# Moving the routing of token runs 0 to 2 from the first expert stage into the last slots of the attention ahead of it

## The reference, cut to what matters

```python
# attention, 8 sequences of 256 tokens, 16 heads of 8
scores = einsum('bhql,bhkl->bhqk', q, k) / sqrt(8)
scores = where(q_ind < k_ind, NEG_INF, scores)
ctx = einsum('bhqk,bhkl->bhql', softmax(scores), v)   # then @ out_w + out_b
# expert layer: x is normed first; every expert is silu(h @ g.T) * (h @ u.T) @ d of width 352
logits = x @ wr.T + rb                                # 7 routed experts
scores, idx = top_k(softmax(logits), 2)
scores = scores / scores.sum(-1)
out = shared_expert(x) + sum_e w[e] * expert_e(x)
```

## Time and profile before

| what | value |
|---|---|
| median of 3 runs | 1063.21 us (1061.97 to 1065.6) |
| span of the profiled execution | 1093.7 us |
| its own time beside the span | none is given; the span stands 30.5 us over the median |
| PE, DVE, ACT, POOL busy | 87%, 67%, 51%, 43% of the span |
| attention of layer 0 | 0 to 182.2 us |
| expert stage of layer 0, last slot starts | 182.2 us, 349.8 us |

### The profile page before, as it was taken

One profiled execution on the slowest core, in us unless ns is written; L12 is line 12 of the kernel. 1 busy time (PEld: TensorE's weight loads), 2 busy tenths in 40 slices (PEclk: granted clock), 3 DMA queues, 4 the chain that ended last, 5 costly groups with the idle time before them and its releaser, 6 DMA issues. The chain is left out here.

```text
span 1093.7 us, 24314 instructions
## 1 busy us (share of the span) xinstructions
PE 946.4 (87%) x8249; PEld 744.2 (68%) x8264; DVE 730.1 (67%) x2020; ACT 561.5 (51%) x1164; POOL 472.5 (43%) x528
## 2 busy tenths in 40 slices
PE   6999987867999399999879999999999967768990
PEld 5666666767998376666566667777666856768990
DVE  4677654545666577887577566766676778755664
ACT  2667762223665247787545554544545435225662
POOL 2355664444344522322364333343456432774443
PEclk9999997889999599999999999999999979988995
DMA  9221110021121312422120011101111720022214
GB/s 304 64 63 54 54 56 1 27 58 38 44 58 31 77 41 61 133 62 79 43 60 21 2 41 41 42 13 29 41 41 41 281 54 1 30 67 58 57 45 116
DMA packets 80754, 66.46 MB, mean 61 GB/s; under 512 B 6706, under 2 KB 73441, under 8 KB 80251
## 3 DMA queue, kind: packets, MB, share of 16 engines
q1 hardware_dynamic: 71899, 54.34, 17.6%
q0 software_dynamic: 4512, 8.47, 2.3%
q10 hardware_dynamic: 4224, 2.10, 0.8%
HBM read 38.76 MB, written 26.58 MB: 60 GB/s over the span
## 5 line engine op out<-in xcount | busy, mean ns | idle before, releaser
L822 DVE TENSOR_REDUCE a_rowmax<-a_banks 128x4 f32<-128x1024 f32 (+1 forms) x112 | 136.8, 1222 | 50.3 <-PE a_banks L1205 19.6
L2771 POOL TENSOR_TENSOR a_both<-a_probs 128x512 f32<-128x512 f32 x64 | 86.4, 1350 | 142.5 <-ACT a_probs L3080 142.4
L1024 ACT ACTIVATE a_probs<-a_banks 128x1024 f32<-128x1024 f32 x112 | 114.9, 1026 | 56.4 <-PE a_banks L1191 44.5
L1800 POOL DMA_INDIRECT acc<-m_result,m_yb x77 | 75.5, 980 | 105.7 <-DVE m_result L2119 58.9
L3080 ACT ACTIVATE a_probs<-a_banks 128x1024 f32<-128x1024 f32 x64 | 65.6, 1025 | 85.5 <-PE a_banks L3253 85.5
L1793 POOL DMA_INDIRECT rows<-m_yrow,m_idx x64 | 64.1, 1001 | 57.2 <-issue 22.6
L2929 DVE TENSOR_REDUCE a_rowmax<-a_banks 128x4 f32<-128x1024 f32 x64 | 77.7, 1219 | 13.1 <-PE a_banks L3226 13.1
L2262 ACT ACTIVATE m_gate<-m_banks 128x352 f32<-128x352 f32 (+1 forms) x93 | 42.9, 462 | 77.2 <-PE m_banks L2471 60.7
L3269 PE MATMUL a_banks<-a_probs,a_V 128*64 128x256 f32 x512 | 69.4, 392 | 0.0
L2497 PE MATMUL m_banks<-e_down,m_hT_hi 128*128 (+2 forms) x231 | 65.2, 350 | 0.6 <-DVE m_hT_lo L2102 0.6
L691 POOL TENSOR_SCALAR_AFFINE_SELECT a_probs<-a_probs 128x512 f32<-128x512 f32 (+1 forms) x48 | 37.9, 790 | 63.8 <-ACT a_probs L1024 63.7
(11 more groups left out here) (418 smaller groups left out, 2778.4 us busy)
## 6 DMA issues: line engine op xcount, KB each, us to landing
rows<-fill SPq DMA_DIRECT2D x16, 520.0 KB, 4.3
a_factor<-recip_rows SPq DMA_DIRECT2D x28, 256.0 KB, 4.6
rows<-fill SPq DMA_DIRECT2D x15, 455.0 KB, 4.0
m_yb<-rows SPq DMA_DIRECT2D x77, 65.0 KB
a_expert<-in_experts SPq DMA_DIRECT2D x16, 257.5 KB
e_gu_lo<-in_gu SPq DMA_DIRECT2D x1, 2736.0 KB
e_last_row<-in_last_rows SPq DMA_DIRECT2D x1, 2736.0 KB
e_gu_lo<-in_gu SPq DMA_DIRECT2D x1, 2464.0 KB, 12.3
```

The source lines that it names most:

```text
L822: nc.vector.reduce_max(o, src, AX).then_inc(rowmax_ready, 1)
L1024: nc.scalar.activation(probs[h][:, k, :, :], ps[:, 4:6, :], ACT.Exp, scale=SCALE).then_inc(exp_done, 1)
L1800: nc.gpsimd.indirect_dma_start(acc.rearrange("k n d -> (k n) d"), bass.IndirectOffsetOnAxis(yb[b % YB][:, P:P + 1].bitcast(U32), 0), resul ...
L2771: nc.gpsimd.tensor_tensor(both[u % 4][:, :, :], p[:, :, 0, :], p[:, :, 1, :], ALU.add).then_inc(both_ready, 1)
```

## The change

A class `Routing` takes the routing out of `experts`. The attention gets it as `route`, and calls, after each `step(s, u)`, a `route_step(s, u)` on every engine:

```diff
+            def route_step(s, u):
+                if (s, u) == (2, 3):
+                    route.constants(pool)
+                if (s, u) in ((8, 0), (9, 1), (11, 0)):
+                    route.power(pool, ((8, 0), (9, 1), (11, 0)).index((s, u)))
+                sends = {(10, 3): (0, 0), (10, 4): (0, 1), (10, 5): (0, 2), (11, 1): (0, 3), (11, 2): (1, 0), (11, 4): (1, 1),
+                         (11, 5): (1, 2)}
+                if (s, u) in sends:
+                    r, t = sends[(s, u)]
+                    route.send(pool, r, [t])
...
+                at_step = {(4, 5): ["tables"], (7, 4): ["stats 0"], (8, 3): ["norm 0"], (9, 0): ["stats 1"], (9, 2): ["norm 1"],
+                           (9, 4): ["scores 0"], (9, 5): ["choices 0"], (10, 1): ["share 0"], (10, 2): ["scores 1"],
+                           (10, 3): ["spots 0", "choices 1"], (10, 4): ["stats 2"], (10, 5): ["share 1", "spots 1"],
+                           (11, 1): ["norm 2"], (11, 4): ["scores 2"], (11, 5): ["choices 2"], (12, 2): ["share 2", "spots 2"]}
...
-            LAST = {SEQS + 1: {1: 3, 3: 1, 4: 2}, SEQS + 2: {1: 3, 3: 1, 4: 2}} if causal else \
+            LAST = {} if causal else \
...
-                    if causal and s == LASTS + 4 and u == MP:
-                        ahead.power(pool)
...
-FIRST_SHARED = 10
+FIRST_SHARED = 12
...
+EARLY_RUNS = {0: RUNS - 1, 3: RUNS // 2}
...
+    last = RUNS - 1
+    behind = {-1: [("norm", last)], 0: [("early", 0)], 1: [("router", last)], 2: [("score", last)],
+              4: [("gap", last), ("one_hot", last)], 6: [("spot", last), ("share", last), ("send", last)], 9: [("map", 0)]}
+    events = [("send", last - 2, 3), ("stats", last), ("send", last - 1)]
+    for n in range(-2, W + 2):
+        events += [("slot", n)] + behind.get(n, [])
+    return events
```

More of the change, by code:

```diff
@@ L957, in ffn_step, with route_step @@
                         ffn.normed(dve, 7)
+            def route_step(s, u):
+                at_step = {(4, 5): ["tables"], (7, 4): ["stats 0"], (8, 3): ["norm 0"], (9, 0): ["stats 1"], (9, 2): ["norm 1"],
[3 rows of a table added]
+                for what in at_step.get((s, u), []):
+                    if what == "tables":
+                        dve.wait_ge(g.loaded["moe0"], 16)
+                        route.regions(dve)
+                        route.tables(dve)
+                        continue
+                    what, r = what.split()
+                    r = int(r)
+                    if what == "stats":
+                        dve.wait_ge(x_done, 2 * r + 2)
+                        route.stats(dve, r)
+                    if what == "norm":
+                        route.norm(dve, r)
+                    if what == "scores":
+                        route.scores(dve, r)
+                    if what == "choices":
+                        route.gaps(dve, r)
+                        route.choices(dve, r)
+                    if what == "share":
+                        route.share(dve, r)
+                    if what == "spots":
+                        route.spots(dve, r)
             if rope:
@@ L968, in _ @@
                         ffn_step(s, u)
[L969 to L974, removed]
+                    if route:
+                        route_step(s, u)
             if ffn_key:
@@ L1813, in _ @@
                     power("c_out", r, c_out_var, c_out_rstd)
-                if kind == "stats" and r == 0 and not by_distance:
-                    pool.sem_inc(in_rstd, 1)
-                elif kind == "stats":
-                    power("in", r, in_var, in_rstd)
+                if kind == "stats":
+                    route.power(pool, r)
                 if kind == "ahead_power" and not by_distance:
@@ L3590, in load_rest @@
                 load_x(sp, k)
[L3591 removed]
+            load_small(sp, ("moe0",))
             load_experts(sp, 0, a["gu0"], a["down0"], w0)
[L3594 to L3598 removed]
+        attention8(nc, g, 0, "att0", prefetch=load_rest, spare=w0, route=route0)
+        g.w |= {k: high.sb(f"w_{k}", a[k].shape) for k in ("att1", "ffn1")}
+        experts(nc, g, 0, "moe0", w0, route=route0, load_next=lambda sp: load_small(sp, ("att1", "ffn1")))
         first.close()
```

812 lines of the change are left out of this document (462 added, 350 removed).

## The result

Over 16 runs of each kernel the changed one takes 1072.51 us (1066.16 to 1085.48) and the one before 1065.40 (1058.79 to 1071.89). The ratio is 1.0065, with a 95% interval of 1.0045 to 1.0085: **0.65% slower, 7 us**. I had forecast 1055, in a range of 1043 to 1069, and "slower" at 0.18.

What follows compares the result with a forecast made beforehand. PE alone was taken to bound the expert stage, a chain through all engines the attention's end. Tail +15.7, slot 0 +6.8, slot 53 -17.1 profiled or -7 timed; -8 taken: 1063.2 - 8 = 1055 us, range 1043 to 1069.

Steps and rivals of the forecast that it cites:

- the steps in slots 2 to 9: Attention slots 2 to 9: routing steps on DVE, mostly hidden behind its waits on PE, cost 1.0 us together (0 to 3).
- the ring: Attention: what the twelve removed idle matmuls filled; they weren't on the path, at most 0.3 us each.
- First send: Attention tail: the first row DMA can start once `idx` is there, taken as 166.3 us.
- The tail behind it: Attention's end: POOL never free, 17.6 us of sends, 10.5 of old work, 1.2 of waiting; x complete at 196.6.
- Start of the stage: Expert stage start: 1.3 us after x, then 5.3 for two sends, power, norm and turn; slot 0 at 203.2.
- The 53 slots: Expert stage after slot 0: 114.5 us at PE's pace plus 15 (6 to 22); slot 53 at 332.7.
- The 6 us for ACT's stalls: Expert stage: 18 sends still go out while slots run, at 0.5 us of ACT stall each; 6 of 9 us taken.
- Profile and median: Whole kernel: ACT's stalls, about 30 us, lie in the profiled execution and hardly in timed ones; gain taken as 8.
- their being real: Rival for the whole kernel: ACT's stalls are in timed runs too, so the whole 17 us shows, 1046; chance 0.19.
- B: Rival, attention tail: a chain and not POOL-bound, sends delay awaited work, 13 us more, 1068; chance 0.24.
- The port rule (C): Rival, attention tail: DVE lengthens sends, 7.8 us; with table loads, both in part, 1061 to 1063; chance 0.10.
- The table loads: Attention, ACT: Tanh between exponentials could need six loads, 7.7 us, half hidden, +4 to 1059; the skill expects none.

Runs made afterwards that it cites:

- e1: The kernel before without its twelve unneeded matmuls of slots 9 and 10, nothing else changed; 1076.53 us, ratio 1.0089 to the kernel before.
- e4: The changed kernel plus 89 unneeded matmuls in slots 9 to 12, all 14 sends kept in the attention; 1067.13 us, ratio 1.0020 to the kernel before.
- e0: The kernel before, unchanged, profiled a second time; 1059.9 us for that one execution.
- e11: The changed kernel with e6's order and e10's 51 matmuls, all 14 sends in the attention; 1062.91 us, ratio 0.9975 to the kernel before.
- e3: The changed kernel with all 14 sends moved out of the attention into the expert stage; 1075.42 us, ratio 1.0074 to the kernel before.
- e6: The changed kernel with the last norm's statistics and power ahead of two row DMAs at the expert stage's start; 1071.77 us, ratio 1.0078 to the kernel before.
- e7: The changed kernel with the edits of e4 and e6 together; 1065.19 us, ratio 1.0011 to the kernel before.
- e5: The changed kernel with the edits of e3 and e4 together; 1069.42 us, ratio 1.0035 to the kernel before.
- e10: The changed kernel with 6 sends in the attention for 14 and 51 unneeded matmuls in slots 10 to 12; 1057.76 us, ratio 0.9926 to the kernel before.
- e12: The kernel before with e10's 29 matmuls of slots 9 and 10 in place of its own twelve; 1074.40 us, ratio 1.0074 to the kernel before.
- e9: The changed kernel with 6 sends in the attention for 14 and e4's 89 matmuls; 1061.14 us, ratio 0.9954 to the kernel before.

## Why the prediction was wrong

**The step that failed** is the term for the steps in slots 2 to 9: 1.0 us for all of them, and nothing for the clock, since "the twelve idle matmuls that go weren't on the path, at most 0.3 us each for the ring that they filled". I priced a removed matmul at its own duration. In the kernel before, the twelve were worth the clock of the 36 us behind them (0.50 from 146 to 170 us, 0.56 to 182): 13.6 us in x complete and 0.9% of the time (e1). In the changed kernel they aren't all of it: putting them back gives 3.6 us of x, holding the clock by more of them 5.6 (e4). The earlier trace rows had a sign: slot 10 before stood at 0.80 already, so the clock had fallen there once, and the change took matmuls out and put waits in.

For timed runs I forecast slot 53 to come 7 us earlier, and against e0 the last product came 10.7 later. Of these nearly 18 us, 11.5 lie ahead of the end of x (+27.2 for +15.7), 3.4 between it and slot 0 (-5.5 for -8.9), and 3 in the 53 slots (-11.0 for -14).

*First send.* Forecast 166.3, measured 176.9 with the clock low, 170.2 to 171.3 with it held (e4, e11). So the clock makes 5.5 to 6.7 of these 10.6 us. Four to five are left with it up. They can be the routing steps of DVE and PE, at more than the 1.0 us that I gave them, or the unneeded matmuls that hold the clock in these runs; no run tells them apart.

*The tail behind it.* Forecast 29.3 us from the first send to the end (17.6 + 10.5 + 1.2); measured 28.6 in the changed kernel and 28.5 in e4 and e11. The sum was right, and so was its mechanism: POOL has no idle time of over 1 us in it, at either clock. What the forecast didn't have is the second limit close behind: with the clock low and no send at all, x is complete only 3.7 us earlier (e3). The forecast end of 196.6 was missed by 8.8, and all of that ahead of the first send.

*Start of the stage.* Forecast 6.6 us from x complete to slot 0, measured 9.4. POOL stands idle for 3.8 us before its first send, put down to "issue" in the row of 209.24, where I had 1.3 us from the addition to the stage, and the power waits behind that and two sends. The two sends were worth 1.7 us (e6, e7). The clock of this stretch made little of it: 9.1 us in e4, where it was higher (0.82 for 0.68).

*The 53 slots.* Forecast 114.5 + 15 = 129.5, to the first product of slot 53; measured 119.7 (120.2 to its second one). The 6 us for ACT's stalls didn't come, nor most of the 9 for run 3 and the clock. The forecast for timed runs, 23 us of excess before and 9 after, was near the truth: 16 and 5 (130.7 and 119.7 to the first product, less 114.5). That slot 53 of the profiled execution came at 334.5, so near the forecast of 332.7, is luck: it started 11.6 us late and took 9.8 us less. The early blocks never waited for rows in the changed kernel, as forecast; in e3 they do. This part of the change does what it says, and so it does in every other version of the changed kernel (118.7 to 118.9 us), but for e3 and e5 with 128.

*Profile and median.* That the stalls of ACT belonged to the one profiled execution was right, and I gave it the greater weight; but I also gave 0.19 to their being real.

*The rivals.* B (slower, 1068) had the right sign and size and named x complete after 203 as its sign; its mechanism, sends ahead of masks and norms in a chain, explains no more than the 3.7 us that come back when all of them are gone at the low clock (e3). Its wait for `idx` did come, 10.6 us and not the 2 that it gave, and for the most part by the clock; so its number was near by luck. The queue shows its price once the clock is held (e10 against e11), and the waiting of the turn of run 2 for DVE's norm, which waits for POOL's power, does show in the changed kernel:

```profile
191.09 1.09 PE L1963 MATMUL a_banks<-ident,m_yrow 128*128 128x128 f32 x4 [4.98 <-DVE m_yrow L1777]
```

No rival had the clock. The port rule (C): by the Trainium skill (SBUF — State Buffer, "SBUF: two separate sides") a send beside DVE work in a two-port mode should have been longer. The fourteen took 0.96 to 1.03 us but for the first one (1.18), and behind the first pair the two of a pair started 1.29 to 1.34 apart, as sends do in the expert stage before (0.95 to 1.04, the first 1.18); so no run here shows it, and whether any of this DVE work is of that mode isn't shown either. The table loads didn't come either: there is one, at 202.19 us, behind the last Tanh, as the kernel before has one at 172.4 (e0); the trace agrees with the Trainium skill (ScalarE: Activation LUTs, "Table sets: the hidden batching unit").

**What stays open.** How much of the 4 us by which the first send is late with the clock held is DVE's share of the routing, how much PE's, and how much the added matmuls'; how far the waits of the routing, without the loss of the twelve, bring the clock down; and what makes it fall earlier in one execution than in the next (e6), or in e5.

## What to carry to other kernels

Matmuls that nobody reads can be the most valuable ones: before they are removed, or waits are put beside them, read the granted clock of the stretch behind them, and price them by that stretch at half the clock, not by their own duration. Their place counts as well as their number (e12), so the granted clock has to be read again after any move. Where two limits are nearly level (here PE's chain at the low clock and POOL's queue), mending one shows little, and only both together (e9, e10) tell what each is worth. And one profiled execution is a sample: set its own time beside the timed runs before taking its stalls for the kernel's.

## What the runs showed of the hardware

Once the clock had fallen, a PE that the profile calls busy nearly all the time didn't have it back at once. From 146 to 162 us the changed kernel's PE was busy for 7.78 and 7.02 of 8 us and stayed at 0.50, which is 1.2 GHz; it came to 0.71 for one stretch of 8 us and was at 0.50 again from 170 to 182. The kernel before, with 6.89, 7.32 and 7.27 busy us from 138 to 162, stayed at 1.00 (e0). The two busy times aren't alike: at 0.50 there are 58 and 51 matmuls in the 8 us, at 1.00 there are 88 to 94.

The same program differed by 13 us between executions (e6, 1059.8 to 1072.9 in the runs behind its ratio), and e10 only by 3.8 (1056.9 to 1060.8). But e4 and e9, whose profiles hold the clock to 170 us as well, spread over 7.6 and 14.4 us, and e1, whose clock is low, only over 3.1 (1074.6 to 1077.7), so it isn't the held clock that makes a kernel steady.

The first profiled execution had stalls of ACT of up to 9.9 us without a releaser; the second one of the same kernel had none in either expert stage.
